# Decoder stack on one core: the first stage loads its weights through two buffers, sums by single columns, and takes over the zero stores

## The reference

```python
x = inputs * rsqrt(mean(inputs * inputs, -1) + EPS) * norm_weight
probs = softmax(mean(x, axis=1) @ router_w.T + router_b)      # [8 batches, 8 experts]
W_hg = einsum('be,ekd->bkd', probs, w_hg)                     # 8 experts x 512 x 256
W_out = einsum('be,eod->bod', probs, w_out)                   # 8 experts x 256 x 256
hg = einsum('bsd,bkd->bsk', x, W_hg); hidden, gate = split(hg)
... recurrence over the 512 tokens gives h ...
out = einsum('bsk,bok->bso', h, W_out) + inputs
```

## Time and profile before

| | before |
|---|---|
| median of 3 runs | 2355.41 us |
| the profiled execution's own time | 2355.41 us |
| its span | 2353.4 us |
| PE busy | 1923.2 us (82%) |
| DVE busy | 1340.0 us (57%) |
| ACT busy | 943.7 us (40%) |
| POOL busy | 627.3 us (27%) |
| mean granted TensorE clock | 0.91 of full |

### The profile page before, as it was taken

The page is one execution under the profiler, slowest core; times in us unless marked ns, Lnnn a source line. Parts: engine busy times, 40 slices in busy tenths (PEclk is TensorE's granted clock), DMA queues, the critical chain, the costliest instruction groups (busy, mean ns, idle before and its releaser), DMA issues. The chain is left out here.

```text
span 2353.4 us, 30152 instructions
## 1 busy us (share of the span) xinstructions
PE 1923.2 (82%) x8625; PEld 1154.0 (49%) x8625; DVE 1340.0 (57%) x3286; ACT 943.7 (40%) x2525; POOL 627.3 (27%) x806
## 2 busy tenths in 40 slices
PE   7785857888888888748849999994665999689998
PEld 5453524455545444426635665652444666444443
DVE  2482448898989889724422222226772455546666
ACT  3322659888988888613312222211111333100000
POOL 2000025555555555404420000006542011100000
PEclk9897979999999999967659999996887999989999
DMA  5524631121112122022231213204332021110110
GB/s 194 204 85 152 239 123 50 55 66 48 60 58 63 50 63 64 22 87 81 80 133 63 80 64 107 72 27 131 117 98 83 33 85 63 47 45 26 36 36 18
DMA packets 173999, 188.56 MB, mean 80 GB/s; under 512 B 18596, under 2 KB 157083, under 8 KB 172864
## 3 DMA queue, kind: packets, MB, share of 16 engines
q1 hardware_dynamic: 166592, 162.76, 21.1%
q0 software_dynamic: 6144, 16.18, 2.0%
q10 hardware_dynamic: 1152, 8.39, 0.8%
HBM read 114.48 MB, written 67.11 MB: 77 GB/s over the span
## 5 line engine op out<-in xcount | busy, mean ns | idle before, releaser
L746 POOL TENSOR_SCALAR xa_probs<-xa_probs,xa_rinv 128x512 f32<-128x512 f32 x512 | 344.6, 692 | 293.9 <-DVE xa_rinv L791 293.9
L911 PE MATMUL xa_ps_t<-xa_ident,xa_probs 128*128 128x128 f32 x2048 | 327.1, 286 | 59.3 <-POOL xa_probs L746 53.4
L764 ACT ACTIVATE xa_probs<-xa_ps_s,xa_nmax 128x512 f32<-128x512 f32 x512 | 351.9, 708 | 26.5 <-DVE xa_nmax L795 26.1
L911 PEld LDWEIGHTS xa_ps_t<-xa_ident,xa_probs 128*128 128x128 f32 x2048 | 234.4, 144 | 239.0 <-POOL xa_probs L746 84.0
L795 DVE TENSOR_REDUCE xa_nmax<-xa_ps_s 128x2 f32<-128x1024 f32 x256 | 307.2, 1200 | 39.7 <-PE xa_ps_s L903 38.1
L681 ACT ACTIVATE xa_probT<-xa_ps_t 128x512 f32<-128x512 f32 x368 | 226.5, 621 | 61.7 <-PE xa_ps_t L911 52.9
L2341 PE MATMUL ga_ps_e<-ga_ew,ga_xT 128*128 128x512 f32 x512 | 235.0, 608 | 0.0
L903 PE MATMUL xa_ps_s<-xa_k,xa_q 96*128 96x512 bf16 x512 | 159.5, 394 | 53.5 <-ACT xa_probs L764 33.0
L2281 DVE SCALAR_TENSOR_TENSOR ga_acc<-ga_ps_e,ga_gate,ga_acc 128x256 f32<-128x256 f32 x256 | 123.9, 484 | 79.0 <-PE ga_ps_e L2341 70.9
L2341 PEld LDWEIGHTS ga_ps_e<-ga_ew,ga_xT 128*128 128x128 f32 x512 | 95.2, 193 | 114.3 <-issue 103.0
L1406 ACT ACTIVATE ex_hid<-ex_ps_g 128x512 f32<-128x512 f32 x64 | 38.3, 598 | 254.5 <-PE ex_ps_u L1459 254.5
(11 more groups left out here) (361 smaller groups left out, 3127.2 us busy)
## 6 DMA issues: line engine op xcount, KB each, us to landing
xa_q<-scratch_qk_parts SPq DMA_DIRECT2D x192, 64.0 KB
xa_k<-scratch_qk_parts SPq DMA_DIRECT2D x192, 64.0 KB
scratch_buf<-rec_zeros ACTq DMA_DIRECT2D x8, 1024.0 KB, 11.8
ex_x<-scratch_buf SPq DMA_DIRECT2D x16, 512.0 KB, 4.3
scratch_results<-ex_out SPq DMA_DIRECT2D x16, 512.0 KB, 3.1
mix_chunk<-in_L_mix_w SPq DMA_DIRECT2D x12, 512.0 KB, 8.7
scratch_qk_parts<-proj_partsq SPq DMA_DIRECT2D x8, 768.0 KB, 4.4
scratch_qk_parts<-proj_partsk SPq DMA_DIRECT2D x8, 768.0 KB, 6.0
```

The costliest lines, as they stand in the source:

```text
L746: ins = pool.tensor_scalar(probs[h % NP][:, t, :], probs[h % NP][:, t, :], rinv[h % 2][:, t:t + 1], 1.0, ALU.mult, ALU.mult)
L764: ins = act.activation(probs[h % NP][:, t, :], ps_s[j][:, t % 2, :], ACT.Exp, bias=nmax[h % 2][:, t:t + 1], accum_out=rsum[h % 2][:, t:t + 1])
L911: ins = pe.transpose(ps_t[t % 2][:, i * P:(i + 1) * P], probs[(h - 2) % NP][:, i, t * P:(t + 1) * P], ident[:, :])
```

## The change

The change touches `stage_mix` and the zero stores of `stage_rec`.

1. The 12 chunk buffers become two. SP loads chunk g only when `mixed` has reached g + 1. PE raises `mixed` by 2 once `blocks` is ready, and by 1 after each group, so the first two loads wait for `blocks`, and each later one for the group that used its buffer.
2. The three lists of groups on PE, DVE and ACT, and SP's list of loads, become loops of 6 rounds with two groups each; the waits compare with a register.
3. The sum over tokens is turned around: x is now the 128-column weights and the scales `inv_all` are one moving column. That is 8 matmuls a batch, 64 in all (128 records). The result already has channels on partitions, so `wide`, its fill and its copies on POOL, the copy of the sum on DVE and the two turns on PE are gone.
4. The zero tile is filled by POOL in `stage_mix`. ACT issues the 8 zero stores there, after its squares and ahead of its exponential, and waits for them at the end of `stage_mix`. `stage_rec` has neither.

```diff
-        chunk = [r.sb(f"chunk{g}", [P, C, D]) for g in range(G)]
-        wide = r.sb("wide", [P, B, T, B])
+        chunk = [r.sb(f"chunk{u}", [P, C, D]) for u in range(2)]
@@ block.sync
-            for g in range(G):
-                sp.dma_start(chunk[g][:, :, :], a["L0_mix_w"][g].rearrange("p (c d) -> p c d", c=C)).then_inc(w_ld[g], 16)
+            with sp.Fori(0, G // 2) as i:
+                for u in range(2):
+                    g = 2 * i + u
+                    sp.wait_ge(mixed, g + 1)
+                    sp.dma_start(chunk[u][:, :, :], a["L0_mix_w"][g].rearrange("p (c d) -> p c d", c=C)).then_inc(w_ld[u], 16)
@@ block.scalar
+            act.wait_ge(zero_up, 1)
+            buf = a["buf"].rearrange("(n p r) d -> n p (r d)", p=P, r=2048 // D)
+            for n in range(buf.shape[0]):
+                act.dma_start(buf[n], zeros[:, :]).then_inc(zero_st, 16)
             act.wait_ge(soft_v, 4)
             act.activation(ex[:, :], lg[:, :], ACT.Exp, bias=nmax[:, :], accum_out=esum[:, :]).then_inc(soft_s, 1)
...
+            act.wait_ge(zero_st, 16 * buf.shape[0])
@@ block.gpsimd
-            pool.memset(wide[:, :, :, :], 0.0).then_inc(const_up, 1)
+            pool.memset(zeros[:, :], 0.0).then_inc(zero_up, 1)
             for b in range(B):
                 pool.wait_ge(msq_up, b + 1)
                 pool.tensor_tensor(inv_all[:, b, :], msq[:, b, :], mhalf[:, :], ALU.pow).then_inc(inv_up, 1)
-                pool.wait_ge(inv_up, b + 1)
-                pool.tensor_copy(wide[:, b, :, b], inv_all[:, b, :]).then_inc(wide_up, 1)
@@ block.vector
-            dve.wait_ge(mean_up, 1)
-            dve.tensor_copy(mean[:, :], ps_sum[:, :]).then_inc(mean_up, 1)
-            dve.wait_ge(mean_up, 3)
+            dve.wait_ge(mean_up, B)
...
@@ block.tensor
-            pe.wait_ge(const_up, 6)
             for b in range(B):
-                pe.wait_ge(wide_up, b + 1)
-                for t in range(T):
-                    ins = pe.matmul(ps_sum[:, :], wide[:, b, t, :], x_all[:, b, t, :],
-                                    start=(b == 0 and t == 0), stop=(b == B - 1 and t == T - 1))
-            ins.then_inc(mean_up, 1)
-            pe.wait_ge(mean_up, 2)
-            for h in range(DH):
-                ins = pe.transpose(ps_mean[:, h, :], mean[:, h * P:(h + 1) * P], ident[0:B, 0:B])
-            ins.then_inc(mean_up, 1)
+                pe.wait_ge(inv_up, b + 1)
+                for h in range(DH):
+                    for t in range(T):
+                        ins = pe.matmul(ps_mean[:, b, h:h + 1], x_all[:, b, t, h * P:(h + 1) * P], inv_all[:, b, t:t + 1],
+                                        start=(t == 0), stop=(t == T - 1))
+                ins.then_inc(mean_up, 1)
...
             pe.wait_ge(soft_v, 9)
-            for g in range(G):
-                pe.wait_ge(w_ld[g], 16)
-                wait(pe, out_v, g - 1)
-                wait(pe, out_s, g - 1)
...
+            pe.sem_inc(mixed, 2)
+            with pe.Fori(0, G // 2) as i:
+                for u in range(2):
+                    g = 2 * i + u
+                    pe.wait_ge(w_ld[u], i * 16 + 16)
+                    pe.wait_ge(out_v, g + 1)
+                    pe.wait_ge(out_s, g + 1)
...
```

More of the change, by code:

```diff
@@ L75, in stage_mix @@
         mhalf = r.sb("mhalf", [P, T])
-        meanT = r.sb("meanT", [P, DH, B])
+        meanT = r.sb("meanT", [P, B, DH])
         nw = r.sb("nw", [P, DH])
@@ L95, in stage_mix @@
         c_ld = r.sem("c_ld")
-        x_ld, w_ld = [r.sem(f"x_ld{j}") for j in range(B // 2)], [r.sem(f"w_ld{g}") for g in range(G)]
+        x_ld, w_ld = [r.sem(f"x_ld{j}") for j in range(B // 2)], [r.sem(f"w_ld{u}") for u in range(2)]
         ssq_up, msq_up, inv_up, mean_up = (r.sem(n) for n in ("ssq_up", "msq_up", "inv_up", "mean_up"))
@@ L99, in stage_mix @@
         mixed, out_v, out_s = r.sem("mixed"), r.sem("out_v"), r.sem("out_s")
-        wide_up = r.sem("wide_up")
+        zeros = r.sb("zeros", [P, 2048])
+        zero_up, zero_st = r.sem("zero_up"), r.sem("zero_st")
         block = ctx.enter_context(nc.Block())
@@ L178, in _ @@
                               mask[:, :].rearrange("p (o k) -> p o k", o=1).to_broadcast([P, B, KC]), ALU.mult).then_inc(soft_v, 1)
[L179 to L182, removed]
+            dve.sem_inc(out_v, 2)
+            with dve.Fori(0, G // 2) as i:
+                for u in range(2):
+                    g = 2 * i + u
+                    dve.wait_ge(mixed, g + 3)
+                    dve.tensor_copy(w_all[:, :, 0, bass.ds(g * (C * KC), C * KC)].rearrange("p b (c k) -> p b c k", c=C),
+                                    ps_w[u][0][:, :, :, :].rearrange("p c b k -> p b c k")).then_inc(out_v, 1)
         @block.tensor
         def _(pe):
[L186 removed]
             for b in range(B):
[L188 to L196 removed]
+                pe.wait_ge(inv_up, b + 1)
[4 more added lines that the diff above has]
+                ins.then_inc(mean_up, 1)
             pe.wait_ge(soft_v, 2)
             for h in range(DH):
[L199 removed]
+                ins = pe.matmul(ps_small[0:B, 0, 0:E], meanT[:, :, h], rwT[:, h, :], start=(h == 0), stop=(h == DH - 1))
             ins.then_inc(soft_t, 1)
@@ L205, in _ @@
             pe.wait_ge(soft_v, 9)
-            for g in range(G):
-                pe.wait_ge(w_ld[g], 16)
-                wait(pe, out_v, g - 1)
-                wait(pe, out_s, g - 1)
[L210 to L214, removed]
+            pe.sem_inc(mixed, 2)
+            with pe.Fori(0, G // 2) as i:
+                for u in range(2):
+                    g = 2 * i + u
+                    pe.wait_ge(w_ld[u], i * 16 + 16)
+                    pe.wait_ge(out_v, g + 1)
+                    pe.wait_ge(out_s, g + 1)
+                    for h in range(DH):
+                        for c in range(C):
+                            ins = pe.matmul(ps_w[u][h][:, c, :, :].rearrange("p b k -> p (b k)"), chunk[u][:, c, h * P:(h + 1) * P],
+                                            blocks[:, :, :].rearrange("p b k -> p (b k)"), start=True, stop=True)
+                    ins.then_inc(mixed, 1)
 def stage_rec(nc, a, x_all, inv_all, w_all):
@@ L305, in _ @@
             act.wait_ge(c_ld, 16)
[L306 to L309, removed]
             def turned(b, u):
@@ L328, in _ @@
             rounds(act, body)
-            act.wait_ge(zero_st, 16 * buf.shape[0])
         @block.vector
```

17 lines of the change are left out of this document (7 added, 10 removed).

## The result

The changed kernel takes 2372.18 us (median of 4 runs, 2367.06 to 2374.99), the kernel before beside it 2354.38 us (2352.97 to 2359.32). The ratio is 1.0085, with an interval of 1.0063 to 1.0105: slower by about 0.8%.

A forecast was written before the change was run, and what follows sets the result against it. The prediction took TensorE as the busiest engine, 82% of the span, and asked what ends last in the first 85 us. +10.0 + 14.9 - 6.8 = +18.1 us on 2355.4 gave 2373.5 us, range 2366 to 2381.

The forecast's parts named there:

- The sums, +10.0: First stage: 128 one-column records at half clock end at 35.6 instead of 24.76, first group at 39.2 instead of 29.15.
- The two arguments from the earlier trace: Later stage, 8-column matmuls: the clock fell to 0.50 during gapless work, and 3.43 us of them at 0.50 didn't raise it.
- Rival A: First stage: the clock rises in the token sums as before, total +12.5 us, 2368; chance 0.09.
- The mixing, +14.9: First stage: each buffer's load stands between two groups, so mixing takes 38.8 us instead of 23.9; bounds +12 and +19.
- the 0.5 us set aside for a falling clock: Mixing: an allowance for the clock falling now and then, as PE idles 2.2 us in each full-clock cycle.
- The load, 3.6 us: Mixing: time of one 512 KB chunk load from memory, bounds 3.2 and 4.3 us.
- The second stage, -6.8: Second stage: without ACT's store issues its xnT copy comes early, PE starts at 61.0 instead of 67.78; bounds -5 and -10.
- B: Mixing: the clock stays at 0.50 throughout because each group ends in a wait, +10.2 us, 2384; chance 0.09.
- C: Mixing: two buffers are enough and the removed 6.8 us stall decides, -2.9 us, 2352.5; chance 0.03.
- D: Second stage: the stall is not regained because something else is late, total +24.9 us, 2380; chance 0.05.
- The sum: Whole kernel: +10.0 + 14.9 - 6.8 = +18.1 us, giving 2373.5 us.
- the likeliest case: Whole kernel, forecast's mechanism alone, chance 0.68: 2368 (load 3.2 us, second stage -8) to 2380 (load 4.3 us, second stage -5).

The follow-up runs named there:

- sums_only: The kernel before with part 3 of the change alone, the token sums as 64 one-column matmuls: 2365.19 us, ratio 1.0043.
- after_dense_first: The changed kernel with 8 matmuls of 512 columns on zeros ahead of the one-column sums: 2373.12 us, ratio 1.0064.
- sums_128_columns: The kernel before with part 3 alone, but each sum matmul has 128 moving columns, the same scale 128 times: 2358.98 us, ratio 0.9998.
- the second profile: The changed kernel run again without an edit, for another profile and more timed runs: 2373.39 us, ratio 1.0065.
- loads_only: The kernel before with parts 1 and 2 alone, two chunk buffers and loops, loads behind the wait for PE: 2369.84 us, ratio 1.0062.
- after_four_buffers: The changed kernel with four chunk buffers instead of two and rounds of four groups: 2362.32 us, ratio 1.0015.
- zeros_only: The kernel before with part 4 alone, POOL's zero fill and ACT's 8 stores moved to the first stage: 2346.71 us, ratio 0.9959.
- fill_early: The kernel before with POOL's zero fill moved to the first stage, ACT still issuing the stores in the second: 2355.60 us, ratio 0.9992.

## Why the prediction was right, point by point

- **The sums, +10.0: right.** 8.05 to 35.52 against 8.05 to 35.6, the first group possible at 39.05 against 39.2. The two arguments from the earlier trace rows hold on their own: few columns don't raise the clock (`sums_only`, first rise at 45.0), and they don't keep it (`after_dense_first`, fall at 18.1). Rival A is out by both, and `sums_128_columns` shows what it would have been. That ACT's issues cost nothing held too: the exponential came at 36.63, 12 us after the last issue.
- **The stores were issued from 15.54, not from 17.8.** ACT's sequencer takes up a DMA while squares ahead of it in the list are still running (last one at 17.66). It changed nothing here. The issues ended at 24.6, and the last store landed at 39.3 (issued at 23.3, 16.0 us to landing), just as the first chunk was asked for at 39.32. The step had said 39.8, from a later start and a higher speed. In the second profile it was 39.6, beside the first 0.3 us of the first chunk's load.
- **The mixing, +14.9: mechanism right, 1.4 too small.** From `blocks` to the last record it took 40.2 us, not 38.8. The wait for the first load was 4.2 (3.9 predicted), 0.3 of the 1.4. The five cycles 43.26 to 74.65 took 31.4, against 7.6 + 4 x 5.8 + 0.5 = 31.3. The last two groups took 4.57 and not 3.58, the other 1.0. That is the term that was mis-sized most: the loads of a pair are issued a group apart, so PE waits for the last one as well (0.53 us), and each broken-off group runs 2.02 us to the end of its last record, not 1.79. That the cycles fit so well is luck: the 0.5 us set aside for a falling clock stood in for cycles of 5.8 to 6.2 us with loads up to 4.3 us. In the first profile the clock didn't fall at all in the mixing, in the second it did once.
- **The load, 3.6 us: right** (median 3.5, `loads_only` 3.5, `after_four_buffers` 3.7). The estimate of 3.2 us by the Trainium skill's "DMA: Bandwidth & Descriptors", section "Anatomy of one DMA — SWDGE (gpsimd) path", whose fit is for DMAs that GpSimd issues, is less than the shortest measured here, 3.3, where SP issued them.
- **The second stage, -6.8: mechanism right, 2.8 too small.** The stage became 9.6 us shorter, in `zeros_only` 10.1. The step took PE's turns to stand where they had stood, at 57.67 to 59.57. But they had been late themselves, for two reasons hidden behind ACT's stall. In before, DVE's 8 normalizations took 3.84 us, because one of them ran into POOL's fill. First DVE's rows before, with POOL's fill, and then its row after (ns, min/median/max):

```profile
54.73 3.84 DVE L336 TENSOR_SCALAR rec_xn<-x_all,inv_all 128x256 f32<-128x256 f32 x8 [0.93 <-PEq L33]
L336 DVE TENSOR_SCALAR rec_xn<-x_all,inv_all x8: 333/346/1966, 54.7 to 58.2; 128x256 f32<-128x256 f32 x8
55.45 1.94 POOL L298 MEMSET rec_zeros<- 128x2048 f32 x1
```

```profile
L335 DVE TENSOR_SCALAR rec_xn<-x_all,inv_all x8: 339/342/380, 80.9 to 82.8; 128x256 f32<-128x256 f32 x8
```

  One instruction of 1966 ns (55.56 to 57.53) beside a fill of 1.94 us (55.45 to 57.39), and none of that kind once the fill is gone. It is the fourth, the last that PE's first turns wait for. That is 1.6 us for the start of the turns (1.3 us after the stage's start instead of 2.94). And the turns then took 1.06 us instead of 1.90, because the clock was still at 1.00 (until 84.5), while before it had fallen at 57.7: 0.8 us. Together 2.4 of the 2.8 us. `fill_early` shows that the first of them is worth nothing while ACT's issues end last. Of the rest, 0.26 us lie in the first `ps_h` (5.20 us instead of 5.46), and 0.1 I can't place.
- **The clock in the second stage was assumed and not as said.** The step had it at 0.50 "in any case" for as long as before, 13.7 us (57.7 to 71.4). After, that stretch was 3.4 us (84.5 to 87.9): PE came to `ps_h` 0.3 us behind the fall instead of 10.1, and the rise followed 3.1 us later (3.6 before). So the 0.8 us of the turns hang on when the clock falls: in the second profile it fell 0.8 us into the stage, the turns took 1.94 us, and the stage is 125.3 us, 8.9 less than before.
- **The rivals.** B (half clock all through the mixing) is out: the rise at 46.9. C (two buffers are enough) is out: a load takes 3.3 us or more, and PE waits in each cycle. With four buffers its mechanism holds, and the mixing loses little more than the wait for the first load. D (the stall not regained) is out by `zeros_only`.
- **The sum** was +18.1. The traces give +16.6 at the start of the third stage (81.1 + 125.3 in the second profile make +18.3), and the timed medians differ by 17.8. The two errors, +1.4 and -2.8, partly cancel. That the total came so near is in part luck. The lower end of the likeliest case is also off in the prediction's own sum: a load of 3.2 us and -8 in the second stage give 2369.9, not 2368.

## What to carry to other kernels

A long transfer that the engine had hidden behind earlier work is not hidden by two buffers: count whether the work on the other buffers covers the whole turn from release to landing (here 4.2 us against 1.79 us a group; three groups cover it, one doesn't). A float32 matmul with one moving column cost as much here as one with 128, and it left TensorE at half clock, so that 128 times the arithmetic was faster. Move DMA issues out of the list of an engine that is next on the path, and then look for what else stood in their shadow: of the change only that part is worth keeping. Alone it gives 0.41% (0.25 to 0.57), the lowest median of this study.

## What the runs showed of the hardware

- TensorE busy without a gap for 17.1 us at clock 0.50, and a fall from 1.00 in the middle of unbroken one-column work (`after_dense_first`). With 128 columns the clock rose after 3.8 us of the same work.
- Records with a 128 x 128 weight load in float32 cost 0.11 us at full clock and 0.21 at half, with 1 moving column as with 8 or 128 (start to start 0.112 and 0.213 in `after_dense_first`, 0.112 in the 128-column sums; 8 columns in the earlier trace rows).
- A normalization on DVE lasted until POOL's fill beside it was over (1966 ns beside 1.94 us; without the fill 339 to 380 ns). The Trainium skill, "SBUF — State Buffer", section "SBUF: two separate sides", has the two engines share a pair of ports as an exclusive lock that is held for a whole instruction, when VectorE's instruction is in a 2-port mode or, against a GpSimd instruction that reads SBUF, has two inputs there. The trace agrees with the lock; in which mode the normalization ran it doesn't show.
- ACT's sequencer issued a DMA at 15.54 while the squares ahead of it ran until 17.84.
- Issuing five stores of 1 MB in a row took ACT 6.5 us in the changed kernel, 1.3 us each, but seven took 3.65 us in `zeros_only`, 0.5 us each, behind a first one of 2.6; why they differ stays open. A chunk's load takes SP 0.33 us. What stands behind the issues in the list waits for them: in before the last issue ends at 66.33, and `xnT` starts at 66.38.
- 8.4 MB of stores beside 6.3 MB of loads put the chunks' landing from 8.7 to 12.9 us in the median (`zeros_only`), at no cost to PE, because nothing waited for them yet.
